# Last attention of a two-layer decoder: normalised and scaled rows moved from VectorE to ScalarE

## The reference, cut to what matters

```python
def _layernorm(x, axis=-1, eps=1e-05):
    m = jnp.mean(x, axis=axis, keepdims=True)
    v = jnp.var(x, axis=axis, keepdims=True)
    return (x - m) / jnp.sqrt(v + eps)
...
# last attention, input _layernorm(x): q, k, v of 16 heads, then
attn = jax.nn.softmax(scores, axis=-1)
out = jnp.einsum('bhqk,bhkd->bhqd', attn, v)
...
# routed network, input _layernorm(x), and inside it
normed = x / jnp.maximum(jnp.linalg.norm(x, axis=-1, keepdims=True), 1e-12)
s = jnp.einsum('bnd,d->bn', x, routing_token)
```

## Time and profile before

| | |
|---|---|
| Median of 3 runs | 415.9 us (415.44 to 420.87) |
| The profiled execution | 415.38 us, of it 413.6 us from the first to the last instruction |
| PE busy | 371.4 us, 90% of the span |
| DVE busy | 325.2 us, 79% |
| ACT busy | 262.5 us, 63% |
| POOL busy | 148.5 us, 36% |
| Mean granted clock of PE | 0.984 |

### The profile page before, as it was taken

The page is one execution under the profiler, slowest core; times in us unless marked ns, Lnnn a source line. Parts: engine busy times, 40 slices in busy tenths (PEclk is TensorE's granted clock), DMA queues, the critical chain, the costliest instruction groups (busy, mean ns, idle before and its releaser), DMA issues.

```text
span 413.6 us, 9875 instructions
## 1 busy us (share of the span) xinstructions
PE 371.4 (90%) x3392; PEld 230.8 (56%) x3392; DVE 325.2 (79%) x899; ACT 262.5 (63%) x582; POOL 148.5 (36%) x248
## 2 busy tenths in 40 slices
PE   6899999999989888999987898999989989899791
PEld 6775444544434577599877643444444434466591
DVE  7778889998995368056977497999999997649896
ACT  2336888888878555764644126887877787676630
POOL 8515654466000023011124604256466332351120
PEclk9989999999999999999999998999999999999996
DMA  7432233223510000000001340221311200000003
GB/s 217 124 95 54 78 106 78 70 54 99 162 40 2 2 0 3 0 2 2 1 2 26 93 103 12 66 54 41 79 46 41 73 2 2 2 2 1 0 2 101
DMA packets 35734, 20.01 MB, mean 48 GB/s; under 512 B 4054, under 2 KB 34694, under 8 KB 35686
## 3 DMA queue, kind: packets, MB, share of 16 engines
q1 hardware_dynamic: 34886, 17.81, 16.3%
q10 hardware_dynamic: 608, 1.18, 0.8%
q0 software_dynamic: 192, 0.39, 0.3%
HBM read 5.58 MB, written 1.05 MB: 16 GB/s over the span
## 4 chain that ended last, share of the span: by engine, by line
PE 55%; DVE 25%; ACT 7%; issue 7%; POOL 3%; DMA 2%; ACTq 0%; DVEq 0%; POOLq 0%
PE pv_ps L1266 11%; PE s_ps L1220 10%; DVE negmax_sb L851 8%; PE pv_ps L1161 4%; PE s_ps L1321 3%; PE s_ps L1229 3%; DVE late_sb L1092 3%; PE prep_ps L1176 3%; ACT probT_sb L577 3%; PE s_ps L1333 2%; DVE xn_sb L828 2%; POOL rstd_sb L455 2%; PE s_ps L1384 2%; PE s_ps L1539 2%; PE prep_ps L1180 2%
## 5 line engine op out<-in xcount | busy, mean ns | idle before, releaser
L851 DVE TENSOR_REDUCE negmax_sb<-s_ps 128x2 bf16<-128x512 f32 x256 | 164.2, 690 | 22.4 <-PE s_ps L1229 21.7
L577 ACT ACTIVATE probT_sb<-s_ps 128x512 f32<-128x512 f32 x256 | 142.2, 597 | 32.2 <-PE s_ps L1220 29.6
L1220 PE MATMUL s_ps<-stack_sb 63*128 63x256 bf16 x512 | 89.5, 274 | 8.0 <-ACT probT_sb L577 3.1
L1229 PE MATMUL s_ps<-stack_sb 62*128 62x256 bf16 x512 | 90.0, 276 | 1.7 <-DMA stack_sb<-parts_sb 1.7
L1266 PE MATMUL pv_ps<-probT_sb,v_aug_sb 128*32 128x256 f32 x1024 | 69.4, 389 | 0.5 <-ACT probT_sb L577 0.5
L1220 PEld LDWEIGHTS s_ps<-stack_sb 63*128 63x128 bf16 x512 | 30.9, 94 | 63.6 <-ACT probT_sb L577 39.6
L453 POOL TENSOR_SCALAR rstd_sb<-mv_sb 128x2 f32<-128x2 f32 x32 | 7.1, 221 | 117.2 <-DVE mv_sb L820 117.0
L1266 PEld LDWEIGHTS pv_ps<-probT_sb,v_aug_sb 128*32 128x32 f32 x1024 | 26.9, 110 | 26.0 <-issue 14.4
L599 ACT ACTIVATE qkf_sb<-prep_ps,b_qkv_sb 128x256 f32<-128x256 f32 x56 | 23.9, 471 | 21.2 <-PE prep_ps L1180 15.8
L1229 PEld LDWEIGHTS s_ps<-stack_sb 62*128 62x128 bf16 x512 | 30.6, 95 | 5.6 <-DMA stack_sb<-parts_sb 1.9
L1161 PE MATMUL pv_ps<-ident_sb 128*128 128x128 f32 x162 | 29.2, 318 | 4.0 <-POOL ident_bf_sb L438 1.9
(11 more groups left out here) (190 smaller groups left out, 669.3 us busy)
## 6 DMA issues: line engine op xcount, KB each, us to landing
stack_sb<-parts_sb SPq DMA_DIRECT2D x186, 64.0 KB, 2.1
x_all_sb<-x SPq DMA_DIRECT2D x4, 256.0 KB, 2.9
ctxT_sb<-ctxT ACTq DMA_DIRECT2D x2, 512.0 KB, 6.5
f_w_sb<-f_w SPq DMA_DIRECT2D x2, 512.0 KB, 4.3
out<-x_all_sb SPq DMA_DIRECT2D x4, 256.0 KB, 2.4
d_w_sb<-d_w SPq DMA_DIRECT2D x2, 320.0 KB, 3.6
w_att_sb<-w_att SPq DMA_DIRECT2D x2, 256.0 KB, 3.5
stack_sb<-maxrow_sb ACTq DMA_DIRECT2D x32, 4.0 KB
```

Source lines behind the costliest of these rows:

```text
L577: act.activation(probT[:, c % 8], s2_ps[c % 2][:, :, :], ACT.Exp, scale=DH ** -0.5).then_inc(exp_ready, 1)
L851: dve.tensor_reduce(negmax[:, n % 2, :, max_column(max_head(h))], s1_ps[c % 3][:, :, :], axis=AX.X, op=ALU.max, negate=True).then_inc(max_ ...
L1220: i = pe.matmul(s2_ps[c % 2][:, k, :], stack[rows, s3, 1, h // 2, k * P:(k + 1) * P], stack[rows, s3, 0, h // 2, :], start=True, stop=True)
L1229: i = pe.matmul(s1_ps[c % 3][:, k, :], stack[rows, s3, 0, hp, k * P:(k + 1) * P], stack[rows, s3, 1, hp, :], start=True, stop=True)
```

## The change

In the last attention, ACT writes `xn` and (for the batches of steps 10 to 14) `xr`, as Identity with a per-row scale and a per-row bias: `x * rstd + (-mean * rstd)` in place of `(x - mean) * rstd`. POOL makes the bias in two 128x1 instructions after the root, and after `xr_scale`. ACT's `xnT_copy` moves from head 3 to head 4. DVE keeps the layer norms of the first attention and of the middle, and `xr` of the last steps as far as POOL doesn't make it.

```diff
+            def scaled_mean(m):
+                u = item(m) % 2
+                pool.wait_ge(rstd_ready, item(m) + 1)
+                for k in range(NT):
+                    i = pool.tensor_scalar(minus_mean[:, u, k:k + 1], mv[:, u, k, 0:1], rstd[:, u, k:k + 1], -1.0, ALU.mult, ALU.mult)
+                i.then_inc(mean_ready, 1)
+            def scaled_z_mean(b):
+                pool.wait_ge(rn_ready, b + 1)
+                for k in range(NT):
+                    i = pool.tensor_scalar(minus_z_mean[:, b, k:k + 1], z_mv[:, b, k, 0:1], xr_scale[:, b, k:k + 1], -1.0, ALU.mult, ALU.mult)
+                i.then_inc(z_mean_ready, 1)
...
                         rstd_step_(item(n))
+                        if n >= B:
+                            scaled_mean(n)
                     add_bias(n)
                     if lo == B and n >= lo + 5:
                         z_norms(n - lo - 5)
+                        scaled_z_mean(n - lo - 5)
...
+            def ln_apply_last(m):
+                n, u = item(m), item(m) % 2
+                act.wait_ge(mean_ready, m - B - AHEAD_C + 1)
+                act.wait_ge(xnT_psum, n - 1)
+                for k in range(NT):
+                    i = act.activation(xn[:, u, k, :], x_all[:, tiles(n).start + k, :], ACT.Identity, bias=minus_mean[:, u, k:k + 1],
+                                       scale=rstd[:, u, k:k + 1])
+                i.then_inc(xn_ready, 1)
+            def xr_apply_act(b):
+                act.wait_ge(z_mean_ready, b + 1)
+                if b >= 2:
+                    act.wait_ge(xrT_psum, b - 1)
+                for k in range(NT):
+                    i = act.activation(xr[:, b % 2, k, :], x_all[:, last_tiles(b).start + k, :], ACT.Identity, bias=minus_z_mean[:, b, k:k + 1],
+                                       scale=xr_scale[:, b, k:k + 1])
+                i.then_inc(xr_ready, 1)
...
@@ ScalarE, in the loop over h, behind exps, max_copy and place_max
-                        if h == 3 and x is not None:
+                        if h == 2 and lo == B and x is not None:
+                            ln_apply_last(i + 3)
+                        if h == at(lo, 3, 4) and x is not None:
                             xnT_copy(x)
+                        if h == 12 and lo == B and has(i - 2, lo) and i < 2 * B - 1:
+                            xr_apply_act(i - 2 - B)
@@ VectorE, in the loop over h
-                        if h == 2 and ln is not None and ln != 1:
+                        if h == 2 and lo == 0 and ln is not None and ln != 1:
                             ln_apply(ln)
...
-                            if h == 12:
+                            if h == 12 and i == 2 * B - 1:
                                 xr_apply(i - 2 - B)
```

More of the change, by code:

```diff
@@ L108, in build @@
         xn = sb("xn", [P, 2, NT, D])
+        minus_mean = sb("minus_mean", [P, 2, NT])
+        minus_z_mean = sb("minus_z_mean", [P, B, NT])
         xnT = sb("xnT", [P, 2, S])
@@ L247, in build @@
             sem("d_in"), sem("d_folded"), sem("s_tok_ready"), sem("z_stats_ready"), sem("z_mv_ready"), sem("s_raw_ready"), sem("rn_step"), sem("rn_ready"))
+        mean_ready, z_mean_ready = sem("mean_ready"), sem("z_mean_ready")
         mask_ready, others_psum, rank_ready, rank_psum = sem("mask_ready"), sem("others_psum"), sem("rank_ready"), sem("rank_psum")
@@ L559, in _ @@
                 z_norms(b)
+                if b < B - 3:
+                    scaled_z_mean(b)
                 if b < B - 1:
```

## The result

The kernel after took 429.2 us (median of 4 runs, 427.88 to 430.63), against 418.4 us for 4 runs of the kernel before beside it (415.44 to 424.34). The ratio of the two is 1.0325, 95% interval 1.0275 to 1.0375: slower. One of the four runs of before, 424.34 us, fell in the slower state that this chip shows now and then, and the ratio leaves it out, so it is more than 429.2 over 418.4. The profiled execution of the kernel after took 430.63 us, span 428.8 us, mean granted clock 0.968.

The account below looks back on a forecast made before the run. It took TensorE's order with ScalarE's latencies to bound step 9 and VectorE steps 10 on; delays in steps 8 to 14 summed to +4.1 us on 415.4, 419.5, given as 419.7 us (+0.9%), 8 in 10: 412.8 to 424.0.

Parts of the forecast that it names:

- +0.75: Step 11: TensorE transposes the normalised rows at 293.1 instead of 292.35, waiting for ScalarE's rows.
- the clock: Rival, 10%: TensorE's clock falls at the new 1.3 us wait, 1.8 us in each of four steps: 426.8 us.
- The activations: ScalarE's 20 new 128x128 activations with two per-row pointers: 485 ns each, 0.87 us to a pair's end.
- GpSimd's two: GpSimd's two 128x1 instructions for the mean after each root: 0.52 us with the way to ScalarE, bounds 0.35 and 1.5.
- Head 5 released by exponential 3: Step 11: TensorE's head 5 waits for ScalarE's delayed exponential 3 and starts at 293.57 instead of 292.69, +0.88.
- Steps 13 and 14: ScalarE's scaled rows delay exponential 13, for which head 15 waits: +0.57 for step 13, +0.65 for step 14.
- has become the limit: From step 10 on VectorE sets the step, busy 14.40 of 14.52 us in step 11.
- The relief: Rival, 17%: not slower; steps 10 to 12 gain 0.28, 0.28, 0.62, steps 13 and 14 0.51 each: -2.2, 413.2 us.
- Small prices: Rival, 20%: ScalarE's pair takes 0.60 and GpSimd's mean 0.35 us, leaving +1.5 us: 416.9 us.
- It doesn't do what it says: Rival, given no chance: excluded by the diff's order, apart from step 15 and the last rows.

Follow-up runs that it names:

- e11: Kernel after, with ScalarE's copy of the transposed maxima moved ahead of the layer norm's rows in steps 8 to 12: 422.04 us, 1.0165 against before.
- e5: Kernel after, with 8 idle matmuls on TensorE ahead of the transposition of xn in steps 8 to 12: 422.54 us, 1.0153 against before.
- e3: Kernel after, with ScalarE's layer norm rows moved behind exponential 3 and the copy of the maxima: 421.49 us, 1.0159 against before.
- e2: Kernel after, with the layer norm's rows back on VectorE and xnT_copy back at head 3: 416.96 us, 1.0033 against before.
- e6: Kernel after, layer norm rows, transposition, copy, projections at later heads (4, 6, 6, 8), ScalarE scaling xr in steps 10 to 12 only: 416.15 us, 0.9979 against before.
- e8: Kernel after, layer norm rows on ScalarE at head 4, transposition at head 6, all xr on VectorE, GpSimd's means unread: 417.05 us, 1.0003 against before.
- e1: Kernel after, with all xr back on VectorE and only the layer norm's rows on ScalarE: 427.66 us, 1.0311 against before.
- e10: Kernel before, with xr transposed at head 14, ahead of the V projection, in steps 10 to 12: 416.52 us, 1.0029 against before.
- e4: Kernel after, with 13 idle matmuls on TensorE ahead of the transposition of xn in steps 8 to 12: 427.03 us, 1.0311 against before.

## Why the prediction was wrong

The direction was right (slower), the time wasn't: 419.7 predicted, range to 424.0, 429.2 measured. To "slower by over 2%" I had given 0.11.

**The step that failed:** "Now ScalarE stops at 291.35, waits until 292.1, works until 293.0, and TensorE transposes at 293.1 instead of 292.35 (+0.75)." The transposition came 2.31 us behind the start of head 4 in the kernel after (300.64 to 302.95) and 0.79 us behind it before (291.56 to 292.35): +1.52, twice the +0.75. I took the normalised rows to be the only thing that TensorE waits for there, because in step 11 of before they are what came last. The matmul has two conditions, rows and bank, and the sum has no term for the second. Yet it was met only 0.26 us earlier in step 11 of before, and in step 9 of before it was the recorded releaser (the row at 264.38 above): reading that step's row as well would have shown it. The change put the first (0.88) in front of the second in one in-order queue, so both moved, and the second ended last, an exponential and a copy later. e11 takes exactly this out: the transposition comes 1.67 us behind head 4 (294.21 to 295.88), +0.88. Its table column differs from e5's, where the copy is late and the clock holds in steps 9 to 12, by 0.12, 0.69, 0.62, 0.62 and 0.63 in steps 8 to 12: 2.7 us.

**The rival that came true on top:** the clock, to which I gave 10%. Its trigger was priced with a wait of 1.3 us (where it indeed stayed away: e3 and e11, steps 9 to 12) and the wait became 1.7 to 2.4. A fall was sized somewhat high: I had "1.8 in each of four steps", 7.3 in all; it fell in three of the four (9, 11 and 12), and the fills of e5 recover 1.3 to 1.5 in each, 4.2 in all. Step 8 has a fall in before already.

The 11.95 us of the stage are thus 4.65 (e11, what I had priced) + 2.64 (e5 less e11, the bank) + 4.66 (after less e5: the clock in steps 9, 11 and 12 4.16, and 0.50 in step 8, where the clock fell in both). That is a split by three kernels, and its terms would share the total differently in another order.

**What was right**, read from e11, where the bank isn't in the way:

| step | 8 | 9 | 10 | 11 | 12 | 13 | 14 | sum |
|---|---|---|---|---|---|---|---|---|
| predicted | 0.84 | 0.72 | 0.56 | 0.56 | 0.22 | 0.57 | 0.65 | 4.1 |
| e11 | 0.93 | 0.84 | 0.60 | 0.60 | 0.24 | 0.74 | 0.70 | 4.65 |

Step 8's agreement is partly luck: before and e11 both have a fall of the clock in it, and the same step of before alone varies by more than 2 us with the clock (last section).

- The activations: groups of ACT by form of the kernel after, whole span. 485 predicted for one, 0.87 for a pair; 485 and 480 measured, 0.88 for the pair. The figures of the Trainium skill's page "ScalarE: Activation LUTs", section "What ACT_TABLE_LOAD costs", give an estimate of 479, and the trace agrees. ScalarE pays nothing for GpSimd's splits: the pair of L626 took 0.86 us at 311.58, beside a split, and 0.88 at 342.27, without one, where VectorE's pair took 1.73 us beside one and 0.51 without, counted to VectorE's next instruction.

```profile
L617 ACT ACTIVATE xn_sb<-x_all_sb,minus_mean_sb,rstd_sb 128x128 f32<-128x128 f32 x10 | 4.4, 485 | 4.9 <-POOL minus_mean_sb L465 4.9
L626 ACT ACTIVATE xr_sb<-x_all_sb,minus_z_mean_sb,xr_scale_sb 128x128 f32<-128x128 f32 x10 | 4.3, 480 | 0.1
```

- GpSimd's two: I took 0.52 from the end of the root to ScalarE, the gap ahead of them included. The rows show 0.63 (299.92 + 0.73 = 300.65 to 301.28): 0.1 too low, in each of five layer norms.
- Head 5 released by exponential 3: the rows of e11 don't show that releaser. Head 5 follows the transposition at once (296.27), since the transposition and the exponential both come 0.9 us late. The size, +0.88 there and about 0.6 at the end of the step, stood.
- Steps 13 and 14: head 15 waits for exponential 13, for 0.54 us, as written. The steps grew by 0.73 and 0.67 where I had 0.57 and 0.65. PE timeline of the kernel after:

```profile
343.69 0.28 PE L1265 MATMUL s_ps<-stack_sb 63*128 63x256 bf16 x1 [0.54 <-ACT probT_sb L600]
```

- One premise wasn't right: VectorE "has become the limit" from step 10 on. Steps 10 and 11 kept their length in e2, e6 and e8, in step 11 with 0.6 to 1.6 us less work on VectorE; only step 12 gained. The relief, a rival of 17%, was smaller than I had it for the same reason: e6 has the relief without the new wait, and wins 0.35 in step 12, where I had -0.62, and nothing in 10 and 11, where I had -0.28 each.

"Small prices" falls with the measured sizes (0.88 for the pair, not 0.60; 0.63 for the mean, not 0.35). "It doesn't do what it says" falls with the profile.

## What to carry to other kernels

Before moving work onto an in-order queue, list for each instruction behind it not only who reads its result but who needs the buffer that it empties; a matmul's recorded releaser is only the latest of its conditions. Here the next one was 0.26 us behind it in one step, and was itself the releaser in another, so read the row of every step. Then ask what TensorE's clock does with the longer wait: in steps 9, 11 and 12 the falls cost 1.3 to 1.5 us each, and all the rest of the change, by e5, 0.9 to 1.5. And an engine that is busy for 99% of a step is worth relieving only by what the next limit leaves: in steps 10 and 11 it was nothing, with TensorE busy for 13.66 of 14.52 us, which the window's PE column showed beforehand.

## What the runs showed of the hardware

- The length of a wait alone didn't tell whether the clock falls. In the kernel after it fell at waits of 1.69 and 1.92 us and not at one of 1.96; e1 has the same waits in steps 9 and 10 and the opposite, no fall at 1.69 and one at 1.95. In e3 and e11 it fell at none of the waits of 1.05 to 1.31. Windows of e1, behind the waits of steps 9 and 10:

```profile
270.00:272.00 2.00, 2.00 (x27) 1.21 (x20) 1.37 (x3) 1.35 (x4) 0.00 (x0) 1.00 0.36 85
286.00:288.00 2.00, 2.00 (x17) 0.87 (x10) 0.72 (x2) 0.75 (x2) 0.00 (x0) 0.50 0.29 70
```

  Windows of e11, step 11, the wait and what follows it:

```profile
294.00:296.00 2.00, 0.72 (x8) 0.30 (x7) 2.00 (x8) 1.40 (x5) 0.84 (x4) 1.00 0.42 101
296.00:298.00 2.00, 2.00 (x30) 0.89 (x29) 1.35 (x3) 1.46 (x4) 1.55 (x3) 1.00 0.34 79
```

  The Trainium skill's page "TensorE: Matmul & The Clock Gate", section "HAM oscillation — how this bites in real kernels", tells of a matmul kernel whose wait for each next slice, a DMA and longer than any wait here, lowers the clock every time, so that the work behind it starts slow. The kernel after and e1 agree in four of five steps each; "every time" they don't show.
- The same work with the same wait can go either way. Step 8 of e2 is that of the kernel before on every engine but GpSimd, which makes a mean that nobody reads there. TensorE's wait at `xn`'s transposition is 0.85 us in both. In e2 TensorE stood as in the earlier trace rows, and went on at 2.4 GHz, where before it had 1.2. The step took 12.14 us instead of 13.67, so this fall cost 1.5 us. In e10, whose step 8 has the very instructions of before, the clock was 0.50 from 250 to 256, and the step took 14.66. Windows of e2, step 8 (its head 0 is at 247.78):

```profile
250.00:252.00 2.00, 0.56 (x7) 0.33 (x6) 1.95 (x5) 0.68 (x2) 1.75 (x5) 1.00 0.14 33
252.00:254.00 2.00, 2.00 (x30) 0.80 (x29) 1.53 (x4) 1.42 (x4) 0.57 (x1) 1.00 0.04 10
```

- One idle product of two 128x128 identities in f32 took 0.24 us at 2.4 GHz (3.17 us for the 13 of e4, which the trace counts as 26), so a fill can be sized from the wait that it is to cover.
- GpSimd can lengthen VectorE's work from a distance. Step 14 took 12.38 us before, 12.39 in e6, 12.69 in e8 and 12.68 in e1; in the last two GpSimd makes a mean for `xr` that nobody reads. It is two 128x1 instructions, 0.51 us, and they push GpSimd's addition to `x` (L532) into VectorE's scaled rows at the end of step 13. The pair then takes 0.90 us instead of 0.59, and VectorE is 0.3 late all through step 14. The two rows of e8, then that of e6, where the addition had ended at 335.48:

```profile
327.99 0.73 POOL L532 TENSOR_TENSOR x_all_sb<-x_all_sb,d_b_sb 128x256 f32<-128x256 f32 x1
328.16 0.90 DVE L1008 TENSOR_SCALAR xr_sb<-x_all_sb,z_mv_sb,xr_scale_sb 128x128 f32<-128x128 f32 x2
...
335.53 0.59 DVE L1008 TENSOR_SCALAR xr_sb<-x_all_sb,z_mv_sb,xr_scale_sb 128x128 f32<-128x128 f32 x2
```
